# The last expert stage of a two-layer transformer kernel, moved into the attention's block of instructions

## The chip, the cores and the metric

The kernel runs on one core of a Trainium2 chip. The metric is the time of the whole kernel in microseconds of the device. The engines are TensorE (PE), VectorE (DVE), ScalarE (ACT), GpSimd (POOL) and SyncE (SP); each takes its own instructions in order and waits for the others by semaphores.

## What is computed

Four residual layers run over x, which is 4 batches of 512 rows by 512:

```python
x = x + tanh(g_xattn[0]) * _L0_xattn_ref(_layernorm(x), ...)
x = x + tanh(g_ffn[0])   * _L0_ffn_ref(_layernorm(x), ...)
x = x + tanh(g_xattn[1]) * _L1_xattn_ref(_layernorm(x), ctx, ...)   # attention, 32 heads of 16
x = x + tanh(g_ffn[1])   * _L1_ffn_ref(_layernorm(x), router_w, w1, w2, w3)
```

Only the last two matter here. The attention rotates queries and keys, takes a softmax over 512 keys, and projects by Wout. The last layer routes each row to two of eight experts with an inner size of 128:

```python
top_scores, selected = top_k(x_flat @ router_w.T, 2); top_scores = softmax(top_scores)
h = silu(xb @ w1[e]) * (xb @ w3[e])          # bfloat16 operands
out = sum over the two experts e of top_score[e] * (h @ w2[e])
```

The kernel computes all eight experts for every row and weighs them by gates that are zero for six of them.

## The kernel before

X (128 partitions by 16 tiles by 512) stays in SBUF throughout. Each layer is a function with its own block of instructions and its own SBUF buffers. A block begins when every engine has finished the one before.

`attention` (L1787) works on 16 units: unit (b, c) is 8 heads of batch b. An order written by hand sets everything. `turns` runs turn(b, c) for b from -1 to 3 and c from 0 to 3, and then turn(4, 0). A turn has 8 steps, each with two slots (slot 2n and 2n+1 belong to step n). In every step PE computes four score tiles of 128 keys by 512 queries (L2138), two before a slot and two after it, and ACT takes the exp of each (L2241); two PSUM banks hold the scores, so each score waits for the exp two before it. PE also takes products with the values (L2168), and for later units score rows whose maxima DVE takes (L2155, L2394). Small jobs go into the slots, as `jobs` lists them, and share PSUM bank 7: "x" transposes normalized rows, which ACT copies to xT (L2079, L2211); "q" projects queries; "m" turns maxima; "o" and "a" turn the attention's output (L2095, L2100) and "p" projects it with Wout (L2107), after which DVE adds it to X (L2384). PE starts a job only when the one before it is done (the table DONE). In the last two turns before (4, 0) much is missing: turn (3, 3) has neither "x", "q" nor "m" and no maxima, and turn (3, 2) has maxima in its first half alone. Turn (4, 0) has only the end of the last unit and sixteen "p" matmuls on four banks.

For each unit POOL stores the maxima and loads them again in another layout (L2056, L2065); the first scores of the unit wait for that load. SP loads keys, values and queries one to three turns ahead.

`l1_ffn` (L2403) is the last block. SP loads the router's weights (L2472). POOL makes constants and issues 17 loads of the experts' weights that turn float32 into bfloat16 on the way (L2488, L2489). DVE takes the row statistics and normalizes batches 0 and 1 (L2530, L2533, L2545), ACT the square roots (L2620). PE turns the normalized rows (L2689), ACT copies them to xT (L2632), POOL casts them to xb (L2496). PE multiplies by the router (L2695), ACT copies (L2637), PE sums the parts (L2701), DVE chooses two experts and makes the gates (L2561 to L2578) with one exp on ACT (L2624). These are the `first_jobs`. Then the loop over 16 tiles: two times `up` (L2715), silu (L2644), product (L2586), weighing by the gates on POOL (L2505), transposes (L2726), their copy (L2650), `down` (L2736), the sum into X (L2591) and the store. The next batch's "x", "l" and "s" jobs lie between these as `side_jobs`.

## Time and profile before

| | |
|---|---|
| median of 3 runs | 1400.13 us (1398.43 to 1401.13) |
| the profiled execution | 1398.27 us, of which the span is 1396.6 us |
| busy: PE, DVE, ACT, POOL | 83%, 62%, 47%, 30% |
| mean granted TensorE clock | 0.930 of full |
| attention's last x added | 1250.7 us |
| first expert matmul | 1273.2 us |

The span reaches from the first instruction to the last. Times in rows are microseconds from its start. The shares of busy time are averages over stages that differ; the stretch between the attention and the experts is read by itself.

### The profile page before, as it was taken

How to read it: one execution, taken by the hardware profiler on the slowest of the kernel's cores; microseconds unless marked ns; L12 is line 12 of the kernel's file. 1: busy time of each engine (PE TensorE's matmuls, PEld its weight loads, DVE VectorE, ACT ScalarE, POOL GpSimd, SP SyncE). 2: the span in 40 equal slices, each digit the busy share in tenths (PEclk: the TensorE clock that was granted, in tenths of full speed). 3: DMA queues.
4: the chain of work that ended last, by engine and by line, in shares of the span. 5: the costliest groups of instructions: out<-in, count | busy, mean ns of one | idle time of the engine just before them, and what ended most of it. 6: DMA issues, size and time to landing. Idle time of an engine off the chain costs nothing. (4 is left out here: it accounts for less than half of the span.)

```text
span 1396.6 us, 16561 instructions
## 1 busy us (share of the span) xinstructions
PE 1165.5 (83%) x5256; PEld 504.7 (36%) x5317; DVE 860.0 (62%) x1325; ACT 654.6 (47%) x1147; POOL 413.2 (30%) x479
## 2 busy tenths in 40 slices
PE   5775875999799999963459988998999999876897
PEld 3443432555444444431013222222322222223453
DVE  7899875214245555315798887778777777226543
ACT  2554452555322222241347666556655556724543
POOL 3475470010132222113334432222222220015332
...
DMA packets 106356, 141.58 MB, mean 101 GB/s; under 512 B 20788, under 2 KB 75572, under 8 KB 106280
## 3 DMA queue, kind: packets, MB, share of 16 engines
...
## 5 line engine op out<-in xcount | busy, mean ns | idle before, releaser
L2394 DVE TENSOR_REDUCE a_top<-PS 128x2 f32<-128x1024 f32 x256 | 308.4, 1222 | 94.8 <-PE PS L2155 90.8
L2241 ACT ACTIVATE a_E<-PS 128x512 f32<-128x512 f32 x512 | 277.7, 596 | 150.0 <-PE PS L2138 149.8
L2138 PE MATMUL PS<-a_Q,a_K 99*128 99x512 bf16 (+1 forms) x469 | 157.0, 386 | 16.6 <-ACT a_E L2241 6.2
L2155 PE MATMUL PS<-a_K,a_Q 64*128 64x512 bf16 x512 | 104.2, 405 | 48.9 <-DVE a_top L2394 29.6
L1367 PE MATMUL PS<-f_W,f_GT 128*128 x312 | 141.6, 597 | 0.0
L2168 PE MATMUL PS<-a_E,a_V 128*32 128x512 f32 x1024 | 136.9, 607 | 0.4 <-ACT a_E L2241 0.4
L2138 PEld LDWEIGHTS PS<-a_Q,a_K 99*128 99x128 bf16 (+1 forms) x512 | 44.2, 97 | 155.4 <-ACT a_E L2241 105.4
L1771 POOL TENSOR_TENSOR a_qf<-a_qf,a_tab 128x512 f32<-128x512 f32 x15 | 19.1, 1270 | 269.3 <-DVE a_swapped L2338 269.3
L1423 DVE TENSOR_TENSOR f_H<-f_SG,PS 128x256 f32<-128x256 f32 x39 | 16.4, 421 | 125.2 <-ACT f_SG L1407 125.2
L1367 PEld LDWEIGHTS PS<-f_W,f_GT 128*128 128x128 f32 x312 | 56.9, 192 | 57.2 <-issue 57.2
L2155 PEld LDWEIGHTS PS<-a_K,a_Q 64*128 64x128 bf16 x512 | 24.7, 93 | 141.9 <-issue 72.4
L2083 PE MATMUL PS<-a_xT,a_wq 128*128 128x512 f32 x128 | 73.9, 675 | 2.1 <-ACT a_xT L2211 0.8
L1386 PE MATMUL PS<-f_W,f_HT 128*128 x156 | 73.2, 593 | 0.0
L2107 PE MATMUL PS<-a_wo,a_attnT 128*128 128x512 f32 x128 | 66.8, 626 | 0.8 <-ACT a_attnT L2231 0.8
L1407 ACT ACTIVATE f_SG<-PS 128x256 f32<-128x256 f32 x39 | 15.0, 384 | 110.0 <-PE PS L1367 110.0
L2715 PE MATMUL PS<-f_W,f_xb 128*128 128x512 bf16 x249 | 62.2, 392 | 0.6 <-issue 0.2
L953 PE MATMUL PS<-f_W,f0r_xT 128*128 128x512 f32 x128 | 58.3, 598 | 0.0
L2505 POOL TENSOR_TENSOR f_H<-f_HF,f_gates 128x512 bf16<-128x512 f32 x32 | 33.3, 1039 | 73.9 <-DVE f_HF L2586 73.9
L1413 ACT COPY f_Y<-PS 128x512 f32<-128x512 f32 x39 | 22.8, 585 | 60.4 <-PE PS L1386 60.4
L2586 DVE TENSOR_TENSOR f_HF<-f_SG,PS 128x512 f32<-128x512 f32 x32 | 22.0, 688 | 47.3 <-ACT f_SG L2644 47.2
L1330 POOL COPY f_idx<-f_token_of 128x1 int32 (+1 forms) x39 | 13.1, 336 | 125.1 <-PE PS L1347 118.0
L1333 POOL DMA_INDIRECT f_G<-f_xn,f_idx x39 | 41.4, 1061 | 29.5 <-POOL f_idx L1330 29.5
...
## 6 DMA issues: line engine op xcount, KB each, us to landing
...
```

Source lines behind the costliest of these rows:

```text
L953: last = nc.tensor.matmul(PS[:, 5, 0:2 * I], xT[b % 2][:, c, t * P:(t + 1) * P], W13[:, E, c, :], start=(c == 0), stop=(c == DC - 1))
L1333: pool.indirect_dma_start(out=G[k][:], out_offset=None, in_=xn_dram, in_offset=bass.IndirectOffsetOnAxis(ap=idx[:, k:k + 1].bitcast(U32), ...
L1367: last = nc.tensor.matmul(PS[:, 2 + k % 2, 0:2 * I], GT[k][:, c, :], W13[:, bass.ds(e, 1), c, :].rearrange("p a n -> p (a n)"), start=(c = ...
L1386: last = nc.tensor.matmul(PS[:, 6 + k % 2, :], HT[k][:, c, :], W2[:, bass.ds(e, 1), c, :].rearrange("p a n -> p (a n)"), start=(c == 0), s ...
L2083: last = nc.tensor.matmul(B, wq[:, extra, c * P:(c + 1) * P], xT[:, extra, :], start=(extra == 0), stop=(extra == DC - 1))
L2107: last = nc.tensor.matmul(bank_of(kind, unit, extra), attnT[b % 2][:, d, t * P:(t + 1) * P], wo[:, d, :], start=(d == 0), stop=(d == DC - 1))
L2138: nc.tensor.matmul(PS[:, 4 + h % 2, :], K6[k][0:rows_, o, head // 2, kt * P:(kt + 1) * P], Q6[k][0:rows_, o, head // 2, :], start=True, st ...
L2155: last = nc.tensor.matmul(PS[:, 2 * pair + o, :], Q6[k][at, o, h // 2, t * P:(t + 1) * P], K6[k][at, o, h // 2, :], start=True, stop=True)
L2168: last = nc.tensor.matmul(PS[32 * h:32 * h + 32, 6, :], V[k][:, kt, (step // 4) * 4 + h, :], E[step % 2][:, h, :], start=(kt == 0), stop=( ...
L2241: nc.scalar.activation(E[step % 2][:, h, :], PS[:, 4 + h % 2, :], ACT.Exp).then_inc(exp_done, 1)
L2394: nc.vector.tensor_reduce(top[:, h - h % 2:h - h % 2 + 2, t], PS[:, 2 * pair:2 * pair + 2, :], AX.X, ALU.max).then_inc(maxed, 1)
L2715: last = nc.tensor.matmul(PS[:, 2 * h + m, :], xb[b % 2][:, c, t * P:(t + 1) * P], W13[:, c, m, h * HE:(h + 1) * HE, :].rearrange("p e i - ...
```

## The change

The last stage becomes a class, `LastStage`, whose parts are called from the attention's block. There is no block of its own any more.

- Buffers: it has none of its own. The up weights lie over Wq and the attention's normalized rows (now one buffer, `early`), the down weights over the keys of ring place 0, the cast rows over the queries of place 0, normalized rows of both batches over place 1, the loop's temporaries over place 2, small things over the rotation table.
- POOL issues 8 weight loads after its work of turn (3, 0), 8 after that of turn (3, 1), and the down weights and the constants after that of turn (3, 2). It casts batch 0's rows in turn (3, 3).
- DVE takes the statistics of batches 0 and 1 at slot 8 of turn (3, 2) and normalizes them at slot 12. ACT takes the square roots at the head of step 6 of that turn.
- In turn (3, 3) the jobs "ex" (slots 0 to 3), "el" (slot 5) and "es" (slot 7) turn the rows, multiply by the router and sum. DVE makes the gates from slot 7 on.
- Then each engine goes on to the loop over tiles (`tensor_main` and so on), whose text is the old one except for two waits of PE for the attention's last sums (`tiles_added`). The last projections use bank 6 in place of bank 0.

```diff
@@ -97,8 +97,7 @@
-        l1_ffn(nc, X, PS, identf, identb, tg, ln_eps, before, ones_b, router_w, w1, w2, w3, out)
+                  (weights, pos, ys, tg[:, 2:3]), (router_w, w1, w2, w3, out))
...
+class LastStage:
...
+    def __init__(self, nc, sem, X, PS, identf, identb, tg, ln_eps, ffn, early, xT, Q6, K6, tab, qf, swapped):
...
+        self.W13 = early[:].rearrange("p a c d -> p (a c d)").bitcast(BF16).rearrange("p (c m e i) -> p c m e i", c=DC, m=2, e=E)
+        self.W2T = K6[0][:].rearrange("p o h s -> p (o h s)").rearrange("p (e d) -> p e d", e=E)
+        self.xT = xT
+        self.xb = [Q6[0][:, k].rearrange("p h s -> p (h s)").rearrange("p (c n) -> p c n", c=DC) for k in range(2)]
+        self.xh = [Z[:].rearrange("p o h s -> p (o h s)").bitcast(F32).rearrange("p (t d) -> p t d", t=TB) for Z in (Q6[1], K6[1])]
+        work = [Q6[2][:].rearrange("p o h s -> p (o h s)"), K6[2][:].rearrange("p o h s -> p (o h s)")]
...
+        self.lT = qf[:, 0, :]
...
+    def sync(self, sp):
+        sp.dma_start(self.rw, self.router_w).then_inc(self.rw_loaded, 16)
...
+    def pool_load_up(self, pool, h):
+        for e in range(h * self.HE, (h + 1) * self.HE):
+            for m, w in enumerate((self.w1, self.w3)):
+                pool.dma_start(self.W13[:, :, m, e, :], w[e].rearrange("(c p) i -> p c i", p=P)).then_inc(self.w13_loaded[h], 16)
...
+    def pool_constants(self, pool):
+        pool.memset(self.rwT, 0.0).then_inc(self.consts_ready, 1)
...
+    def cast(self, pool, b, c):
+        pool.wait_ge(self.xT_ready, b * self.DC + c + 1)
+        if b >= 2:
+            pool.wait_ge(self.up_done, 2 * self.TB * (b - 1))
+        pool.nop(nofuse=True)
+        self.nc.gpsimd.tensor_scalar(self.xb[b % 2][:, c, :], self.xT[:, c, :], 1.0, 0.0, ALU.mult, ALU.add).then_inc(self.xb_ready, 1)
...
+    def constants(self, v):
+        for c in range(self.DC):
...
+    def statistics(self, v, b, n=1):
+        tiles = range(b * self.TB, (b + n) * self.TB)
+        done = b * self.TB
+        for t in tiles:
+            self.nc.vector.bn_stats(self.stats[:, t % (2 * self.TB), :], self.X[:, t, :]).then_inc(self.steps_norm, 1)
+        v.wait_ge(self.steps_norm, done + n * self.TB)
+        for t in tiles:
...
+    def normalize(self, v, b):
+        if b >= 2:
...
+    def choose(self, v, b):
...
+    def root(self, act, b, n=2):
+        act.wait_ge(self.var_ready, b + n)
+        self.nc.scalar.activation(self.sd[:, self.tiles(b, n)], self.mv[:, self.tiles(b, n), 1], ACT.Sqrt, bias=self.ln_eps[:]).then_inc(self.sd_ready, n)
+    def expo(self, act, b):
+        act.wait_ge(self.shifted_ready, b + 1)
+        self.nc.scalar.activation(self.ex, self.shifted, ACT.Exp).then_inc(self.ex_ready, 1)
+    def take_x(self, act, b, c):
+        if (b, c) == (0, 0):
+            act.wait_ge(self.rw_turned, 1)
+            act.wait_ge(self.consts_ready, 3)
+            self.nc.scalar.copy(self.rwT[:, :, 0:self.E], self.SIDE[:, 0:self.DC * self.E].rearrange("p (c e) -> p c e", e=self.E)).then_inc(self.rwT_ready, 1)
+        act.wait_ge(self.x_turned, b * self.DC + c + 1)
+        if b:
+            act.wait_ge(self.xb_ready, (b - 1) * self.DC + c + 1)
+            act.wait_ge(self.l_done, b)
+        self.nc.scalar.copy(self.xT[:, c, :], self.SIDE).then_inc(self.xT_ready, 1)
...
+    def turn_x(self, pe, b, c):
+        nc = self.nc
+        if (b, c) == (0, 0):
+            pe.wait_ge(self.rw_loaded, 16)
+            for d in range(self.DC):
+                last = nc.tensor.transpose(self.SIDE[:, d * self.E:(d + 1) * self.E], self.rw[:, d * P:(d + 1) * P], self.identf[0:self.E, 0:self.E])
+            last.then_inc(self.rw_turned, 1)
...
+            if b:
+                pe.wait_ge(self.logits_taken, b)
+        else:
+            pe.wait_ge(self.xT_ready, b * self.DC + c)
+        for t in range(self.TB):
+            last = nc.tensor.transpose(self.SIDE[:, t * P:(t + 1) * P], self.xh[b % 2][:, t, c * P:(c + 1) * P], self.identf[:])
...
+    def router(self, pe, b):
...
+    def router_sums(self, pe, b):
...
+    def tensor_main(self, pe, tiles_added):
+        nc, PS, TB, DC, E, HE, NT = self.nc, self.PS, self.TB, self.DC, self.E, self.HE, self.NT
+        def job(kind, b, c):
+            if kind == "x":
+                if (b, c) == (1, 0):
+                    pe.wait_ge(tiles_added, NT - 3)
...
+        def turn_h(j):
+            pe.wait_ge(self.h_ready, 2 * j + 2)
+            if j:
+                pe.wait_ge(self.hT_ready, j)
+            else:
+                pe.wait_ge(tiles_added, NT)
...
+def attention(nc, X, PS, identf, identb, ones_b, tg, ln_eps, tgate, Wq, Wout, bout, tables_dram, k_parts, v_dram, routed,
+              ffn):
...
-        wq = sb("wq", [P, DC, D])
+        early = sb("early", [P, 2, DC, D])
+        wq, xh = early[:, 0], early[:, 1]
...
-        xh = sb("xh", [P, TB, D])
...
+            if (b, c) == (NB - 1, DC - 1):
+                for d in range(DC):
+                    add(d, "ex", (0, 0), d)
+                add(5, "el", (0, 0))
+                add(7, "es", (0, 0))
...
-            return PS[:, (7, 4, 5, 0)[extra[0]], :] if kind == "p" and unit[0] == NB - 1 else PS[:, 7, :]
+            return PS[:, (7, 4, 5, 6)[extra[0]], :] if kind == "p" and unit[0] == NB - 1 else PS[:, 7, :]
...
             turns(sp, turn)
+            sp.wait_ge(parts_ready, NU)
+            f1.sync(sp)
...
+            def load_last_stage(b, c):
+                if (b, c) == (NB - 1, 0):
+                    pool.wait_ge(q_turned, NU)
+                    pool.wait_ge(x_turned, NB * DC)
+                    f1.pool_load_up(pool, 0)
+                if (b, c) == (NB - 1, 1):
+                    f1.pool_load_up(pool, 1)
+                if (b, c) == (NB - 1, 2):
+                    pool.wait_ge(st_done, n_st((NB - 1, 0), 7, 3))
+                    f1.pool_load_down(pool)
+                    pool.wait_ge(parts_ready, NU)
+                    f1.pool_constants(pool)
+                if (b, c) == (NB - 1, DC - 1):
+                    f1.pool_first(pool)
...
+                load_last_stage(b, c)
             turns(pool, turn)
+            f1.pool_main(pool)
...
+                if kind == "ex":
+                    f1.turn_x(pe, b, extra)
+                if kind == "el":
+                    f1.router(pe, b)
+                if kind == "es":
+                    f1.router_sums(pe, b)
...
+                    "a": (aT_ready, lambda u, e: n_unit(u)), "p": (x_added, lambda u, e: u[0] * TB + e[0] + 1),
+                    "ex": (f1.xT_ready, lambda u, e: e + 1), "el": (f1.lT_ready, lambda u, e: 1), "es": (f1.logits_taken, lambda u, e: 1)}
...
             turns(pe, turn)
+            pe.wait_ge(maxed, NU * HU * 2)
+            f1.tensor_main(pe, x_added)
...
+                        if kind == "ex":
+                            f1.take_x(act, unit[0], extra)
+                        if kind == "el":
+                            f1.take_router(act, unit[0])
+                        if kind == "es":
+                            f1.expo(act, unit[0])
...
+                    if (b, c, step) == (NB - 1, 2, 6):
+                        f1.root(act, 0)
                     exps((b, c), step, (0, 1))
...
             turns(act, turn)
+            act.wait_ge(st_done, n_st((NB - 1, 2), 7, 3))
+            f1.scalar_main(act)
...
+                if (b, c) == (NB - 1, 2):
+                    def first_rows():
+                        v.wait_ge(x_added, 2 * TB)
+                        v.wait_ge(parts_ready, NU)
+                        f1.statistics(v, 0, 2)
+                    def first_normalized():
+                        v.wait_ge(st_done, n_st((NB - 1, 1), 7, 3))
+                        f1.row_roots(v, 0)
+                        f1.normalize(v, 0)
+                        f1.normalize(v, 1)
+                    at(8, first_rows)
+                    at(12, first_normalized)
+                if (b, c) == (NB - 1, DC - 1):
+                    def first_gates():
+                        v.wait_ge(qf_ready, NU)
+                        f1.constants(v)
+                        f1.choose(v, 0)
+                    at(7, first_gates)
...
-def l1_ffn(nc, X, PS, identf, identb, tg, ln_eps, before, ones_b, router_w, w1, w2, w3, out):
...
```

The order of instructions shows where the parts went. PE in turn (3, 3), before, from the last "p" of turn (3, 2) to the job "a"; Q_3 and K_3 are scores, E and V values:

```order
L2107 MATMUL PS<-a_wo,a_attnT 128x512
L2138 MATMUL PS<-a_Q_3,a_K_3 128x512 x4
L2168 MATMUL PS<-a_E,a_V 32x512 x4
L2138 MATMUL PS<-a_Q_3,a_K_3 128x512 x4
L2168 MATMUL PS<-a_E,a_V 32x512 x4
L2138 MATMUL PS<-a_Q_3,a_K_3 128x512 x2
L2095 MATMUL PS<-identf,a_OT 128x128 x4
```

The same place on PE in the changed kernel (L2086 turns the router's weights, L2096 the normalized rows, which lie in Q_1):

```order
L2534 MATMUL PS<-a_wo,a_attnT 128x512
L2566 MATMUL PS<-a_Q_3,a_K_3 128x512 x2
L2086 MATMUL PS<-identf,a_tab 128x8 x4
L2096 MATMUL PS<-identf,a_Q_1 128x128 x4
L2566 MATMUL PS<-a_Q_3,a_K_3 128x512 x2
L2596 MATMUL PS<-a_E,a_V 32x512 x4
L2096 MATMUL PS<-identf,a_Q_1 128x128 x4
L2566 MATMUL PS<-a_Q_3,a_K_3 128x512 x2
L2096 MATMUL PS<-identf,a_Q_1 128x128 x4
L2566 MATMUL PS<-a_Q_3,a_K_3 128x512 x2
L2596 MATMUL PS<-a_E,a_V 32x512 x4
L2096 MATMUL PS<-identf,a_Q_1 128x128 x4
```

Four groups of transposes and the turning of the router's weights have moved between the scores. PE at the end of the attention, before, up to the first expert matmuls:

```order
L2107 MATMUL PS<-a_wo,a_attnT 128x512 x16
L1810 UNCONDITIONAL_BRANCH
L2673 UNCONDITIONAL_BRANCH
L2677 MATMUL PS<-identf,f_rw 128x8 x4
L2689 MATMUL PS<-identf,f_xh 128x128 x16
L2695 MATMUL PS<-f_xT,f_rwT 32x512 x4
L2701 MATMUL PS<-f_pick,f_lT 128x8 x4
L2715 MATMUL PS<-f_W,f_xb 128x512 x8
```

And in the changed kernel (L2137 is `up`, with the weights in `early`):

```order
L2534 MATMUL PS<-a_wo,a_attnT 128x512 x16
L2137 MATMUL PS<-a_early,a_Q_0 128x512 x8
L2096 MATMUL PS<-identf,a_K_1 128x128 x4
L2137 MATMUL PS<-a_early,a_Q_0 128x512 x8
L2096 MATMUL PS<-identf,a_K_1 128x128 x4
```

The branch into a new block and 28 matmuls ahead of the first expert matmul are gone from there. ACT in the changed kernel, from step 5 of turn (3, 2) to the choice of batch 0's experts (L2677 the attention's exps, L2020 square root, L2035 copies to xT, L2041 the copy behind the router, L2024 the gates' exp):

```order
L2677 ACTIVATE a_E<-PS 128x512 x4
L2020 ACT_TABLE_LOAD
L2020 ACTIVATE a_tab<-a_tab,ln_eps 128x8
L2677 ACT_TABLE_LOAD
L2677 ACTIVATE a_E<-PS 128x512 x10
L2030 COPY a_tab<-PS 128x4x8
L2035 COPY a_xT<-PS 128x512
L2677 ACTIVATE a_E<-PS 128x512 x2
L2686 COPY a_OT<-PS 128x512
L2035 COPY a_xT<-PS 128x512
L2677 ACTIVATE a_E<-PS 128x512 x2
L2035 COPY a_xT<-PS 128x512
```

Two table loads and a square root now stand between exps of the attention, and the copies between those of turn (3, 3).

## Rows read from the trace of the kernel before

**Rows 1.** Stretches: from:to, length, busy PE PEld DVE ACT POOL (count), clock, DMA, GB/s.

```profile
1178.50:1205.60 27.10, 24.96 (x134) 7.48 (x136) 12.77 (x18) 19.27 (x36) 1.62 (x3) 1.00 0.01 2
1205.60:1231.50 25.90, 23.04 (x119) 6.78 (x123) 2.26 (x6) 18.71 (x35) 0.00 (x0) 1.00 0.00 1
1231.50:1250.00 18.50, 15.96 (x48) 6.83 (x40) 3.57 (x7) 1.17 (x2) 0.00 (x0) 1.00 0.00 0
1250.00:1273.20 23.20, 8.65 (x37) 5.25 (x39) 13.55 (x32) 6.16 (x10) 15.93 (x24) 0.61 1.21 136
```

**Rows 2.** Timeline of PE: start, us, engine, line, out<-in, xcount [idle before <-releaser].

```profile
1235.96 13.97 PE L2107 MATMUL PS<-a_wo,a_attnT 128*128 128x512 f32 x32 [0.77 <-ACT a_attnT L2231]
...
1253.83 0.41 PE L2677 MATMUL PS<-identf,f_rw 8*128 8x8 f32 x4 [3.90 <-DMA f_rw<-in_L_ffn_router_w_dram]
1259.20 1.11 PE L2689 MATMUL PS<-identf,f_xh 128*128 128x128 f32 x4 [4.96 <-DVE f_xh L2545]
...
1268.40 1.93 PE L2695 MATMUL PS<-f_xT,f_rwT 128*32 128x512 f32 x8 [0.77 <-ACT f_xT L2632]
1271.12 1.85 PE L2701 MATMUL PS<-f_pick,f_lT 128*128 128x8 f32 x8 [0.79 <-ACT f_lT L2637]
1273.20 2.85 PE L2715 MATMUL PS<-f_W,f_xb 128*128 128x512 bf16 x7 [0.23 <-issue]
...
1276.32 1.89 PE L2715 MATMUL PS<-f_W,f_xb 128*128 128x512 bf16 x8
1281.06 0.65 PE L2689 MATMUL PS<-identf,f_xh 128*128 128x128 f32 x4 [2.85 <-ACT f_xT L2632]
```

**Rows 3.** Timeline of ACT, around a square root in turn (1, 3).

```profile
959.47 1.28 ACT L2256 ACT_TABLE_LOAD   x1
960.76 0.30 ACT L2256 ACTIVATE a_sd<-a_mv,ln_eps 128x4 f32<-128x4 f32 x1
961.08 1.28 ACT L2241 ACT_TABLE_LOAD   x1
```

**Rows 4.** Timeline of ACT, turns (3, 2) and (3, 3), steps before the tail.

```profile
1195.58 2.15 ACT L2241 ACTIVATE a_E<-PS 128x512 f32<-128x512 f32 x4
1198.45 1.08 ACT L2241 ACTIVATE a_E<-PS 128x512 f32<-128x512 f32 x2 [0.71 <-PE PS L2138]
...
1206.12 2.17 ACT L2241 ACTIVATE a_E<-PS 128x512 f32<-128x512 f32 x4 [1.46 <-PE PS L2138]
...
1212.09 2.17 ACT L2241 ACTIVATE a_E<-PS 128x512 f32<-128x512 f32 x4 [0.72 <-PE PS L2138]
```

**Rows 5.** Timeline of ACT, turn (2, 0), steps 4 and 5 with jobs "x".

```profile
1000.65 0.58 ACT L2211 COPY a_xT<-PS 128x512 f32<-128x512 f32 x1 [0.92 <-PE PS L2079]
1001.13 1.09 ACT L2241 ACTIVATE a_E<-PS 128x512 f32<-128x512 f32 x2
...
1005.02 1.06 ACT L2241 ACTIVATE a_E<-PS 128x512 f32<-128x512 f32 x2
```

**Rows 6.** Timelines of DVE and ACT: "o" of turn (3, 2), and the last stage.

```profile
1196.49 0.26 DVE L2372 RECIPROCAL a_rsum<-PS 128x16 f32<-128x16 f32 x1 [3.44 <-PE PS L2095]
...
1252.97 2.46 DVE L2530 BATCH_NORM_STATS2 f_stats<-X 128x6 f32<-128x512 f32 x4
1255.47 0.38 DVE L2533 BATCH_NORM_AGGREGATE f_mv<-f_stats 128x2 f32<-128x6 f32 x4
...
1262.65 3.31 DVE L2545 TENSOR_SCALAR f_xh<-X,f_mv,f_rstd 128x512 f32<-128x512 f32 x4
...
1273.75 0.23 ACT L2624 ACTIVATE f_ex<-f_shifted 128x32 f32<-128x32 f32 x1 [1.47 <-DVE f_shifted L2564]
```

**Rows 7.** Timeline of POOL: loads of maxima, and the first weight loads.

```profile
1140.63 1.12 POOL L2065 DMA_DIRECT2D a_Q<-a_m_rows  x2 [3.02 <-DMA a_m_rows<-a_mT]
1167.21 0.54 POOL L2056 DMA_DIRECT2D a_m_rows<-a_mT  x1 [25.47 <-ACT a_mT L2222]
...
1252.86 11.96 POOL L2488 DMA_DIRECT2D f_W<-in_L_ffn_w_dram  x16
```

586 lines of the change are left out of this document (267 added, 319 removed).

## The prediction, made before the changed kernel ran

> **What bounds the kernel now.** I read the busy time by stretch first, then the timeline of PE between the attention and the experts, then ACT in the attention's last two units, and last DVE and POOL there. In the table of stretches [rows 1] the reader is to see one poor stretch, 1250.00 to 1273.20: PE is busy for 8.65 of 23.2 us at a granted clock of 0.61, and the DMA share is 1.21. All around it the clock is 1.00. The timeline of PE [rows 2] says what stands there: after the last projections (1235.96 plus 13.97, so 1249.93) PE waits 3.90 us for the router's weights and 4.96 us for the normalized rows, then goes through transposes, router and sums, each waiting for an ACT copy, and starts the first expert matmul at 1273.20. It then runs without a long wait for the weights (0.23 us of "issue"). So the 23.3 us from 1249.93 to 1273.20 are a chain of small steps, with the weight loads of POOL beside it [rows 7].
>
> **What is removed.** In the changed order `up` of tile 0 stands right behind the sixteen projections on PE. All that it needs is made earlier: weights in turns (3, 0) and (3, 1), cast rows in turn (3, 3). The gates are needed only by POOL's weighing. The two waits for the attention's sums hide: the first transposes of batch 1 want 13 of 16 tiles, the first `turn_h` all 16, and DVE's last sum ends under 1 us behind the last projection, while `turn_h` stands behind two `up`. The whole 23.3 us go, block boundary included.
>
> The clock goes with them. The first `up` took 2.85 us, the second, at the full clock, 1.89 us [rows 2]: that is 0.96 us. What follows, PE's 2.85 us of waiting for the copy at 1281.06, stays: the chain of silu, product, statistics of batch 2, root and copy is unchanged, only DVE is no longer busy with gates. So the loop gains 1.0 us, and 1.2 if the clock doesn't dip behind that wait. Removed in all: 24.3 us.
>
> **What is added to the attention, step by step.** There ACT's exps and PE's scores take turns, so what stands between them is on the path, less what was idle.
>
> (1) Square roots at the head of step 6 of turn (3, 2). The same pair of table loads stands in turn (1, 3): from 959.47 to 961.08 plus 1.28, 2.9 us for load, root and load [rows 3]. ACT was idle for 0.71 us before that step [rows 4]. Cost 2.2 us. Is its input there? DVE is free after the maxima are cut (1196.49 less 3.44 of waiting, so 1193.1), and eight tiles of statistics are twice 2.46 plus 0.38, 5.7 us [rows 6], so to 1198.8; ACT wants it at 1195.58 plus 2.15 plus a load of 1.28, at 1199.0. It just is. The statistics stand ahead of "o", which DVE did at 1196.49 [rows 6]; it slips by some 2.3 us, and PE's next job with it to about 1199.7, but the scores then wait for ACT until past 1200.6 anyway: no cost. The normalization is two times up to 3.31 us [rows 6], from 1199.5 to at most 1206.3; DVE's next duty is the sum at 1206 plus 2.2. No cost either. The cover is thin here: 1 us more on DVE would show as 1 us.
>
> The Trainium skill, in "ScalarE: Activation LUTs", section "What ACT_TABLE_LOAD costs", gives 1283 ns for a load and some 2.66 us for a switch with the drain behind it. The trace agrees with the first and not with the second: 1.28 us, and the next instruction starts at once [rows 3]. By the page's figure this step would cost two times 2.66 plus 0.30 less 0.71, an estimate of 4.9 us, and the forecast would be 2.7 us later.
>
> (2) The jobs "ex" in slots 0 to 3 of turn (3, 3), with the router's weights in the first. Step 0 and step 1 took 5.97 us together, 1206.12 to 1212.09 [rows 4]. The nearest row is a step of turn (2, 0) with two "x" jobs: 3.9 us with maxima, 1001.13 to 1005.02 [rows 5]; two of them are 7.8, 1.8 more. Here the router's weights come on top. Following the semaphores: PE turns the router's weights (0.41, [rows 2]), waits for ACT's copy, turns rows (half of 1.11 at the full clock), ACT copies (0.58, [rows 5]) and takes its exps; the next "ex" waits for that copy. I get 8.6 us for the two steps, so 2.6 us more.
>
> (3) "el" in slot 5: PE's 1.93 us were at half clock, so 0.97, then ACT's copy of 0.58, for which step 3 waits. ACT had 0.72 us idle a step [rows 4]. I get 1.4 us with the semaphores. (4) "es" in slot 7: half of 1.85, then DVE's copy, maximum and difference, then ACT's exp. From the end of PE's sums (1272.97) to the end of that exp (1273.75 plus 0.23, [rows 2, 6]) is 1.0 us. 1.9 us in a row, of which ACT's idle time and its running exps hide some: 1.0 us.
>
> Sum: 2.2 + 2.6 + 1.4 + 1.0 = 7.2 us. Bounds: nothing hidden gives 2.9 for (1), 0.6 plus four times (0.56 + 0.58) for (2), 5.2, then 1.9 for (3) with a semaphore's delay, and 1.9 for (4), so 11.9 us. At the other end PE's jobs hide under ACT's work and ACT's copies in its idle time: 0.2 + 5 x 0.58 + 0.23 is 3.3 us of ACT, and five steps have 5 x 0.72, 3.6 us, so only the 2.2 us of (1) stay. I take the value between, since it follows the waits one by one; rows 5 show that such copies do not hide whole.
>
> (5) POOL's issues: 16 in 11.96 us, 6 us in each of two turns [rows 7]. POOL has 25.47 us of waiting ahead of the next store of maxima [rows 7], so it is not late. SP is past its loads for the last unit. (6) Casts, constants, and the bank taken instead of bank 0: nobody waits for POOL there. Cost nothing.
>
> **The sum.** 24.3 less 7.2 is 17.1 us. The profiled execution took 1398.27 us, its span 1396.6, so it would take 1381.2. It was faster than the median by 1.9 us and stands just below the three timed runs; against the median of 1400.13 the same difference gives **1383.0 us**, which I predict.
>
> **Rivals.** (A) The transfers collide. The weights are halves of 2 MB read; the whole took from 1252.86 to 1273, with a DMA share of 1.21 [rows 1, 7], so some 10 us a half. POOL issues each half right behind the loads of maxima (issued 1140.63 to 1141.8, wanted by the scores at about 1149), and if their pieces share engines with the weights they land up to 10.6 us later, at 1152.4: 3 us of waiting, twice. Against it: they are ahead in POOL's order, and the transfers of the last two units are nearly none (share 0.01, [rows 1]). The Trainium skill ("DMA: Bandwidth & Descriptors", "Queues, rings and completion order") says that each DMA engine takes the queues in turn, and one queue in its order: by that the earlier loads lose little. It would give 17.1 less 6.3, so 10.8 us of gain: 1389.3 us.
>
> (B) The handshakes run in series, the upper bound above: 24.3 less 11.9 is 12.4 us: 1387.7 us.
>
> (C) Slower than before: the clock. The new jobs put waits of PE, up to 1.2 us each, into turn (3, 3). PE's work there and in the tail is 23.04 plus 15.96 us, 39 us, in 44.4 us [rows 1]. If the granted clock fell to its lower level (1.2 GHz) at the start of that turn and stayed there, 78 us would be needed: 34 us more, against 17.1, so 1417 us. It decides from about 17 us of PE's full-clock work run at half. Against it: at 23.04 busy of 25.90 us the clock was 1.00 throughout, and the projections run without a gap [rows 1, 2]; the only lower clocks follow stretches in which PE did next to nothing.
>
> (D) The change doesn't do what it says: `up` of tile 0 still waits, for the casts or the weights. POOL would have to be 45 us late; the rows show it idle for 25 us a turn. Or the loop gains more than I count, from DVE and ACT that have less to do. Either is small.
>
> **How the numbers follow.** Forecast, a gain of 12.5 to 22.1 us about 17.1: 0.78. (B) or beyond, down to 11 us: 0.08. (A): 0.08. (C): 0.03. (D): 0.03, half of it on the fast side. The added cost between 2.2 and 11.9 us puts the time between 1378.0 and 1387.7; with (A) it reaches 1389.3, and the three runs spread by about 1 us each way. Range 1378 to 1390. About 0.2% is what a measurement of this kernel tells from no change, 2.8 us: faster 0.96, within it 0.01, slower 0.03.
>
> **What would show it.** In the profile after: the first expert matmul within 0.5 us of the last projection, at about 1257; eight of them in 1.9 us; clock 1.00 from there. ACT's load, root and load in 2.9 us before step 6 of turn (3, 2), the exps following at about 1200.6. Steps 0 and 1 of turn (3, 3) in 8.6 us, steps 2 and 3 in 5.8 plus 2.4. A "p" or a score that waits for DVE in turn (3, 2) would say that the statistics are late; a first score of turns (3, 1) or (3, 2) that waits for a DMA would say (A); a clock below 1.00 before the last projection, (C). The forecast is wrong if turns (3, 2) and (3, 3) together grow by less than 2 or more than 12 us.

## The result, and the profile after

| | before | changed |
|---|---|---|
| median of 5 runs | 1401.13 us (1398.43 to 1403.46) | **1390.31 us** (1388.06 to 1394.82) |
| ratio | | 0.9925, 95% interval 0.9904 to 0.9946 |
| the profiled execution | 1398.27 us, span 1396.6 | 1388.06 us, span 1386.4 |
| busy: PE, DVE, ACT, POOL | 83%, 62%, 47%, 30% | 85%, 62%, 47%, 30% |
| mean granted TensorE clock | 0.930 | 0.931 |

The kernel is faster by about 10.5 us. The prediction had 17.1, and its range ended at 1390.0: the direction was right, the size was not. A second measurement gave 1391.30 us, a ratio of 0.9932 (0.9918 to 0.9946); one slow execution of the kernel before in it, 1902.83 us at a granted clock of 0.60, is not counted.

In the changed kernel L2020 is the square root, L2677 the attention's exps, L2035 the copies to xT, L2566 the scores, L2596 the values, L2534 Wout, L2137 `up`, L2160 `down`, L2057 silu. First the table of stretches of the changed kernel, with the columns of [rows 1]:

```profile
1196.00:1204.00 8.00, 5.32 (x32) 1.59 (x24) 6.69 (x21) 6.59 (x11) 2.96 (x5) 1.00 0.03 7
1204.00:1208.00 4.00, 3.67 (x12) 0.94 (x13) 2.74 (x7) 1.85 (x4) 0.99 (x3) 0.57 0.89 119
...
1247.00:1262.00 15.00, 14.79 (x37) 6.58 (x38) 3.00 (x4) 0.07 (x1) 0.00 (x0) 1.00 0.00 1
1262.00:1275.00 13.00, 8.75 (x46) 4.81 (x44) 5.16 (x13) 7.98 (x11) 3.58 (x5) 0.87 0.00 0
```

The poor stretch at clock 0.61 [rows 1] is gone. A new short one stands at 1204 to 1208, inside turn (3, 2), at a granted clock of 0.57. From 1262 to 1275 the clock is 0.87 with PE busy for 8.75 of 13 us; the loop had such a dip before too, as is shown further down. PE's timeline shows what stands at the old boundary and behind it:

```profile
1247.21 13.97 PE L2534 MATMUL PS<-a_wo,a_attnT 128*128 128x512 f32 x32 [0.77 <-ACT a_attnT L2667]
1261.02 1.89 PE L2137 MATMUL PS<-a_early,a_Q 128*128 128x512 bf16 x8
...
1263.19 1.89 PE L2137 MATMUL PS<-a_early,a_Q 128*128 128x512 bf16 x8
1269.33 1.12 PE L2096 MATMUL PS<-identf,a_K 128*128 128x128 f32 x4 [4.25 <-ACT a_xT L2035]
1270.24 3.04 PE L2137 MATMUL PS<-a_early,a_Q 128*128 128x512 bf16 x8
...
1378.44 3.53 PE L2160 MATMUL PS<-a_K,a_K 128*128 128x512 bf16 x8 [1.10 <-ACT a_K L2063]
```

The first `up` follows the projections with no wait, at full clock, as predicted: compare the rows from 1235.96 to 1273.20 in [rows 2]. PE then waits 4.25 us in the loop instead of 2.85, does its third `up` in 3.04 us, and its last `down` takes 3.53 us. ACT in the attention, and where its tables are loaded:

```profile
1197.67 2.15 ACT L2677 ACTIVATE a_E<-PS 128x512 f32<-128x512 f32 x4
1200.77 1.28 ACT L2020 ACT_TABLE_LOAD   x1 [0.95 <-DVE a_tab L1937]
1202.06 0.30 ACT L2020 ACTIVATE a_tab<-a_tab,ln_eps 128x8 f32<-128x8 f32 x1
1202.38 1.28 ACT L2677 ACT_TABLE_LOAD   x1
1203.68 1.08 ACT L2677 ACTIVATE a_E<-PS 128x512 f32<-128x512 f32 x2
...
1208.82 1.09 ACT L2677 ACTIVATE a_E<-PS 128x512 f32<-128x512 f32 x2 [2.76 <-PE PS L2566]
...
1229.00 0.23 ACT L2024 ACTIVATE a_tab<-a_tab 128x32 f32<-128x32 f32 x1 [1.74 <-DVE a_tab L1971]
...
1262.99 1.28 ACT L2057 ACT_TABLE_LOAD   x1 [15.92 <-PE PS L2137]
1264.29 0.60 ACT L2057 ACTIVATE a_Q<-PS 128x512 f32<-128x512 f32 x1
```

Two loads of tables stand *behind* a wait that belongs to the operation after them: the root's (0.95 us for DVE's variances) and silu's (until PE has done `up`).

**Where the 17.1 went.** The first exp of step 5 of turn (3, 2) is a common point: 1195.58 before [rows 4], 1197.67 after. The kernels differ only behind it on the path, so all is counted from there; the 2.09 us ahead of it are taken up below.

| stretch, from the exps of step 5 on | before | after | difference | predicted |
|---|---|---|---|---|
| to step 6 (roots) | 2.87 | 6.01 | +3.14 | +2.2 |
| from there to step 7 | 3.84 | 5.14 | +1.30 | 0 |
| steps 0 and 1 of turn (3, 3) ("ex") | 5.97 | 8.11 | +2.14 | +2.6 |
| step 2 ("el") | 2.88 | 3.94 | +1.06 | +1.4 |
| step 3 ("es") | 2.89 | 4.44 | +1.55 | +1.0 |
| all to the start of the last projections | 40.38 | 49.54 | +9.16 | +7.2 |
| from their start to the first `up` | 37.24 | 13.81 | -23.43 | -23.3 |
| from the first `up` to the sixth | 19.79 | 20.14 | +0.35 | -1.0 |
| from there to the end of the span | 103.61 | 105.24 | +1.63 | 0 |
| sum | 201.02 | 188.73 | -12.29 | -17.1 |

The change is worth 12.29 us in this pair; 2.09 us less show because the profiled execution was later at step 5 already. Of the missing 4.8 us, 0.94 are the roots, 1.30 a step at a low clock and 2.98 the loop. Against these stand 0.25 that the three kinds of job cost less than predicted and 0.13 that the boundary gave more.

### The profile page after: what moved, and what is told of

Same layout as the page of the kernel before. It is cut to its first block, busy times and chain, and to the rows that moved or that the text cites. A ratio compares the mean times of both kernels' runs of the same rounds, so it can differ in the third digit from the quotient of the medians.

```text
span 1386.4 us, 16598 instructions
## 1 busy us (share of the span) xinstructions
PE 1177.1 (85%) x5316; PEld 503.8 (36%) x5317; DVE 856.9 (62%) x1324; ACT 653.6 (47%) x1146; POOL 414.5 (30%) x479
## 4 chain that ended last, share of the span: by engine, by line
PE 30%; DVE 8%; issue 7%; ACT 6%; POOL 2%; DMA 2%; POOLq 0%; ACTq 0%; DVEq 0%
PE PS L2596 8%; PE PS L2566 6%; PE PS L2510 5%; PE PS L2534 5%; ACT a_E L2677 4%; PE PS L2583 4%; DVE a_top L2854 3%; POOL a_K L1908 1%; DMA a_attnT<-f_y,l_pos 1%; PE PS L2137 1%; DVE a_tab L1934 1%; DVE a_early L2756 1%; PE PS L2160 1%; PE PS L2506 0%; PE PS L2527 0%
## 5 line engine op out<-in xcount | busy, mean ns | idle before, releaser
L2677 ACT ACTIVATE a_E<-PS 128x512 f32<-128x512 f32 x512 | 277.7, 596 | 148.2 <-PE PS L2566 147.9
L2566 PE MATMUL PS<-a_Q,a_K 99*128 99x512 bf16 (+1 forms) x512 | 168.0, 388 | 17.9 <-ACT a_E L2677 7.8
L2596 PE MATMUL PS<-a_E,a_V 128*32 128x512 f32 x1024 | 139.0, 615 | 0.0
L2566 PEld LDWEIGHTS PS<-a_Q,a_K 99*128 99x128 bf16 (+1 forms) x512 | 44.5, 98 | 154.6 <-ACT a_E L2677 102.3
L2510 PE MATMUL PS<-a_xT,a_early 128*128 128x512 f32 x128 | 75.6, 689 | 2.1 <-ACT a_xT L2647 0.8
L2534 PE MATMUL PS<-a_wo,a_attnT 128*128 128x512 f32 x128 | 67.1, 629 | 1.4 <-ACT a_attnT L2667 0.8
L1908 POOL TENSOR_TENSOR a_K<-a_Q,a_tab 128x512 bf16<-128x512 f32 x32 | 33.3, 1041 | 109.0 <-DVE a_Q L1996 109.0
L2137 PE MATMUL PS<-a_early,a_Q 128*128 128x512 bf16 x256 | 61.6, 384 | 0.0
L1996 DVE TENSOR_TENSOR a_Q<-a_Q,PS 128x512 f32<-128x512 f32 x32 | 22.0, 687 | 50.4 <-ACT a_Q L2057 50.4
```

What stands on the lines that cost most here:

```text
L1908: self.nc.gpsimd.tensor_tensor(self.H[j % 2][:, h * HE:(h + 1) * HE, :], self.HF[h], gate, ALU.mult).then_inc(self.h_ready, 1)
L2137: last = nc.tensor.matmul(PS[:, 2 * h + m, :], self.xb[b % 2][:, c, t * P:(t + 1) * P], self.W13[:, c, m, h * HE:(h + 1) * HE, :].rearrang ...
L2510: last = nc.tensor.matmul(B, wq[:, extra, c * P:(c + 1) * P], xT[:, extra, :], start=(extra == 0), stop=(extra == DC - 1))
L2534: last = nc.tensor.matmul(bank_of(kind, unit, extra), attnT[b % 2][:, d, t * P:(t + 1) * P], wo[:, d, :], start=(d == 0), stop=(d == DC - 1))
L2566: nc.tensor.matmul(PS[:, 4 + h % 2, :], K6[k][0:rows_, o, head // 2, kt * P:(kt + 1) * P], Q6[k][0:rows_, o, head // 2, :], start=True, st ...
L2596: last = nc.tensor.matmul(PS[32 * h:32 * h + 32, 6, :], V[k][:, kt, (step // 4) * 4 + h, :], E[step % 2][:, h, :], start=(kt == 0), stop=( ...
```

## Experiments

The figures "from step 5" below are in the same measure as the table. Each kernel is the changed one with one edit, but for the first and the last four.

**The kernel before, a second time.** It asks how much of the difference of 2.09 us ahead of step 5 is the kernel's.

> The kernel before, unchanged, for a second trace. In the traced pair the changed kernel is already 2.1 us late in step 5 of turn (3, 2) of the attention (1197.67 against 1195.58), ahead of every instruction that the change added, weight loads apart. Theory (chance): this is the spread of one execution against another, in the stages that wait for DMAs; then this second trace has that step at 1195.6 plus or minus up to 3 us, and the distance from there to the first expert matmul and to the end is the same within 0.5 us (77.6 and 201.0 us). Rival (layout): the changed buffers cost 2 us ahead of the attention; then this trace stands within 0.7 us of 1195.6, and all changed kernels stand near 1197.7.

1399.99 us, span 1398.3. The exps of step 5:

```profile
1197.30 2.15 ACT L2241 ACTIVATE a_E<-PS 128x512 f32<-128x512 f32 x4
```

That is 1.72 us later than in the first profile [rows 4], while everything from there on is the same to 0.02 us: 40.37 to the projections, 77.62 to the first `up`, 123.38 to the end. So times counted from step 5 compare kernels to some hundredths of a microsecond wherever the clock is the same, and the place of step 5 itself is a matter of the execution. In all thirteen profiles of this study step 5 lies between 1195.6 and 1202.6, and most of that spread stands already at the square root of turn (1, 3), at 960.8 to 967.8 [rows 3], ahead of all instructions that the change or an experiment moves.

**The root counted once.** Its semaphore rises by two at once, for two batches. In the trace above the wait for the variances stands in front of the table load and not of the root. That is the exception: in the changed kernel's whole trace only two other loads stand behind a wait, silu's and one at 9.41 us, and at both the program has two waits in a row. At all other places where an operation has to wait, its load runs first and the operation waits. The edit asks whether the increment by two is the reason here.

```diff
-ACT.Sqrt, bias=self.ln_eps[:]).then_inc(self.sd_ready, n)
+ACT.Sqrt, bias=self.ln_eps[:]).then_inc(self.sd_ready, 1)
...
-        v.wait_ge(self.sd_ready, b + n)
+        v.wait_ge(self.sd_ready, b + n - 1)
```

> The square roots' semaphore is raised once by one in place of by two, and its reader waits for one less; nothing else changes. By that the wait for the variances stands on the square root and the table load goes ahead of it. Theory: in turn (3, 2) the load starts at the end of step 5's exps (1199.8 on the scale of the changed kernel's trace) and no longer waits 0.95 us for DVE, so step 6 begins 5.0 us after the last exps of step 5 began in place of 6.0, and with PE's idle time shorter by 0.9 the clock may not dip (then 1.3 us more are gained by step 7). Rival: DVE is late anyhow, and the gain is below 0.5 us.

1385.01 us in one run. ACT:

```profile
1196.57 2.15 ACT L2677 ACTIVATE a_E<-PS 128x512 f32<-128x512 f32 x4
1198.74 1.28 ACT L2020 ACT_TABLE_LOAD   x1
1200.03 0.30 ACT L2020 ACTIVATE a_tab<-a_tab,ln_eps 128x8 f32<-128x8 f32 x1
1200.35 1.28 ACT L2677 ACT_TABLE_LOAD   x1
1201.65 2.17 ACT L2677 ACTIVATE a_E<-PS 128x512 f32<-128x512 f32 x4
```

The load starts right behind the exps, and step 6 comes 5.08 us behind step 5: 0.93 us less, the 0.95 us of the wait. Against the 2.87 us of the kernel before, load, root and load now cost 2.21 us, the 2.2 us of the prediction. The next step took 3.83 us, not 5.14. Both together put the projections 2.22 us earlier (47.32).

**PE kept at work during the roots.** The table's 1.30 us ahead of step 7 have a granted clock of 0.57 around them. Three causes are possible: the low clock, DVE, which normalizes there, or the load of the down weights, which starts there (119 GB/s from 1204 to 1208). Eight unused matmuls fill PE's wait.

```diff
+                    if (b, c, step) == (NB - 1, 2, 6):
+                        pe.wait_ge(maxed, NU * HU * 2)
+                        for _ in range(8):
+                            nc.tensor.matmul(PS[:, 0, :], K6[2][0:99, 0, 0, 0:P], Q6[2][0:99, 0, 0, :], start=True, stop=True)
                     scores((b, c), step, 2)
```

> Eight matmuls of 128x512 bf16 whose results nobody uses are added on PE in step 6 of turn (3, 2), where it idled for 1.86 us while ACT loads tables; nothing else changes, the square roots' 3.1 us stay. Theory (clock): the granted clock fell to its lower level there because PE did next to nothing for 2 us, the values of that step took 1.94 in place of 1.07 us, and step 7 came 1.3 us late. With PE at work the clock stays at 1.00, the values take 1.07 us and step 7 begins 3.8 to 3.9 us after step 6 in place of 5.14. Rival (weights): the down weights' load, which starts there, slows PE; then the values still take 1.9 us and step 7 stays 5.1 us behind.

1390.76 us. PE, in the changed kernel and then in this one:

```profile
1204.33 1.09 PE L2566 MATMUL PS<-a_Q,a_K 99*128 99x512 bf16 x2 [1.86 <-ACT a_E L2677]
1205.36 1.94 PE L2596 MATMUL PS<-a_E,a_V 128*32 128x512 f32 x8
```

```profile
1204.32 1.89 PE L2609 MATMUL PS<-a_Q,a_K 99*128 99x512 bf16 x8
...
1207.15 1.06 PE L2596 MATMUL PS<-a_E,a_V 128*32 128x512 f32 x8
```

The values matmuls take 1.06 us instead of 1.94, step 6 is where it was (6.00) and step 7 is 3.84 us behind it, the figure of the kernel before. DVE's work and the weights' load are unchanged. So the 1.30 us were the clock, behind a wait of PE of 1.86 us, and neither of the other two had a part. Yet the run as a whole won nothing: its last projections took 15.2 us instead of 13.8 (15.4 as the records stand, but that of one matmul of the first `up` is missing), at a granted clock of 0.73 and 0.70 in the six microseconds from 1246 on. That is a low clock at another place, of which more below.

**The router behind the projections.** Batch 0's turning, router, sums and gates leave turn (3, 3) and stand between the last projection and `up`; weights and rows stay where the change put them.

```diff
-                for d in range(DC):
-                    add(d, "ex", (0, 0), d)
-                add(5, "el", (0, 0))
-                add(7, "es", (0, 0))
...
+            pe.wait_ge(x_added, NT - 3)
+            for d in range(DC):
+                f1.turn_x(pe, 0, d)
+            f1.router(pe, 0)
+            f1.router_sums(pe, 0)
             f1.tensor_main(pe, x_added)
```

> One part of the change undone: batch 0's transposes, router, sums and gates stand behind the last projections on all engines again (as in the kernel before), while weights, statistics, square roots and normalized rows stay in the attention's last batch. Times below are from the start of step 5 of turn (3, 2). Changed kernel: projections at 49.54 us, first expert matmul at 63.35. Theory (the steps add as read): turn (3, 3) is free of its 4.9 us, so projections at 44.8 (43.4 without the clock's dip in turn (3, 2)); then the chain runs at the full clock in 4 x (0.56 + 0.68) + 0.8 + 0.6 + 0.97 + 0.7 + 0.93, some 9 us, so the first expert matmul at 67 to 68: 4 us later than in the changed kernel. Rival (the jobs in the attention hide nothing): it comes at 63.4 or before, and placing them there was worth nothing.

1391.37 us. The projections start 45.12 us behind step 5, 4.42 us earlier than in the changed kernel, so that is what the jobs cost in turn (3, 3). The chain between the last projection and the first `up`:

```profile
1254.95 0.41 PE L2086 MATMUL PS<-identf,a_tab 8*128 8x8 f32 x4
...
1261.56 1.94 PE L2102 MATMUL PS<-a_xT,a_tab 128*32 128x512 f32 x8 [0.68 <-ACT a_xT L2035]
1264.29 1.84 PE L2110 MATMUL PS<-a_tab,a_qf 128*128 128x8 f32 x8 [0.80 <-ACT a_qf L2041]
1265.99 3.38 PE L2137 MATMUL PS<-a_early,a_Q 128*128 128x512 bf16 x8
```

It takes 11.1 us (11.04 by the starts), above the 9 expected, because the clock falls in it: the router's 1.94 us and `up`'s 3.38 us are at the lower level of 1.2 GHz. The first `up` is at 70.06, later than the 67 to 68 that were expected. So moving the router into the attention is worth 70.06 less 63.35, 6.7 us at the first `up`, and all the rest (weights, rows, the block's boundary) 77.62 less 70.06, 7.6 us. The loop gave some back to this kernel (123.71 against 125.38): silu's table could be loaded while the slow `up` ran. The whole is 5.0 us by the profiles (1.67 less than the 6.7).

**Silu's table load.** At the end of the attention ACT has two waits in a row, for the last scores and for the first `up`. One of them is carried by the table load. The first is implied by the exps before it and can go.

```diff
             turns(act, turn)
-            act.wait_ge(st_done, n_st((NB - 1, 2), 7, 3))
             f1.scalar_main(act)
```

> One wait of ACT is left out that earlier waits of ACT already cover, the one on the scores of turn (3, 2) ahead of the loop over tiles; nothing else changes. In the changed kernel the load of silu's table stands behind the wait for the first expert matmuls: PE ends at 1262.91, the load takes 1.28 us, silu starts at 1264.29. Theory (load behind its wait): with one wait in place of two the load goes ahead of it, silu starts about 0.1 us after the matmuls, and the second group of transposes of batch 1 comes at 7.0 us after the first expert matmul in place of 8.3; the loop after tile 4 is 1.3 us nearer. Rival: the load's time is not what sets that place (statistics or copies do), and it moves by less than 0.5 us.

1392.95 us in one run, but in it step 5 was at 1202.59, the latest of all. Counted from the first `up`, the rest took 121.85 us instead of 125.38. ACT now, and the last `down`:

```profile
1252.30 1.28 ACT L2057 ACT_TABLE_LOAD   x1
1271.16 0.60 ACT L2057 ACTIVATE a_Q<-PS 128x512 f32<-128x512 f32 x1 [17.58 <-PE PS L2137]
```

```profile
1384.96 1.90 PE L2160 MATMUL PS<-a_K,a_K 128*128 128x512 bf16 x8 [1.10 <-ACT a_K L2063]
```

The load is done under the projections. The sixth `up` is 1.6 us earlier (1.8 as the records stand, but that of one matmul is missing at the first `up`). PE's wait shrank from 4.25 to 2.92 us, which is the load's 1.28, and the transposes and third `up` behind it were 0.23 us shorter; the last `down` takes 1.90 us as in the kernel before, not 3.53. Here too the projections were slow, by 3.0 us: 0.65 was the clock from 1249 to 1258, against 1.00 in the changed kernel at about the same place.

```profile
1249.00:1258.00 9.00, 6.83 (x15) 3.34 (x16) 0.68 (x2) 2.23 (x3) 0.00 (x0) 0.65 0.01 2
```

```profile
1243.00:1252.00 9.00, 6.53 (x27) 3.03 (x20) 1.79 (x4) 1.17 (x2) 0.00 (x0) 1.00 0.01 2
```

**PE kept at work in the loop.** Twelve unused matmuls behind the second `up`, four ahead of the last `down`.

```diff
+            if j == 0:
+                pe.wait_ge(tiles_added, NT)
+                for _ in range(12):
+                    nc.tensor.matmul(PS[:, 6, :], self.xb[0][:, 0, 0:P], self.W13[:, 0, 0, 0:HE, :].rearrange("p e i -> p (e i)"), start=True, stop=True)
             for one in self.side_jobs(b, t, 1):
                 job(*one)
```

> Twelve matmuls of 128x512 bf16 without use are added behind the second group of tile 0, where PE waits 4.25 us for a copy, and four ahead of the last tile's product, where it waits 1.1 us; nothing else changes. Theory (clock): the lower clock behind those waits goes (the third group of expert matmuls took 3.04 in place of 1.89 us, the last product 3.53 in place of 1.89), so from the first expert matmul to the end it takes 125.4 less 1.2 to 2.8 us: 122.6 to 124.2. Rival: both dips were hidden by other waits; then it stays at 125.4.

1388.34 us. From the first `up` to the end 123.62 us, 1.76 us less than in the changed kernel. Of these, 0.45 stand at the sixth `up`, where the third now takes 1.89 us, and 1.31 behind it. This is the end of the loop:

```profile
1379.07 1.03 PE L2181 MATMUL PS<-a_early,a_Q 128*128 128x512 bf16 x4
1380.34 1.90 PE L2160 MATMUL PS<-a_K,a_K 128*128 128x512 bf16 x8 [0.24 <-ACT a_K L2063]
```

More work on PE made the loop shorter; the `down` that follows the unused matmuls takes 1.90 us. From step 6 to step 7 of turn (3, 2), untouched here, it took 5.49 us, so the slow step came again (5.14 in the changed kernel, 3.84 before).

**The statistics spread over turn (3, 1).** DVE takes one tile's statistics in each of slots 1 to 8 of turn (3, 1), ACT the root before step 7 of it, and the normalization moves to slot 8 of turn (3, 2). It asks whether the roots cost less where more matmuls (those for the maxima) stand beside them.

```diff
+                    for t in range(2 * TB):
+                        at(t + 1, lambda t=t: one_row(t))
+                    at(10, rows_done)
...
-                    if (b, c, step) == (NB - 1, 2, 6):
+                    if (b, c, step) == (NB - 1, 1, 7):
                         f1.root(act, 0)
```

> Statistics of batches 0 and 1 are taken one tile in a slot in turn (3, 1) in place of eight at once in turn (3, 2); the square roots stand ahead of step 7 of turn (3, 1), where ACT waits 1.7 us for PE in every step, and the rows are normalized from slot 8 of turn (3, 2). Theory: in turn (3, 2) steps 5, 6, 7 and the next are as in the kernel before (2.87, 3.84, 3.83 us), which gives back 4.4 us there; turn (3, 1) grows by 2.9 less 1.7, so 1.2 us, plus what 5.7 us of statistics cost DVE, which has 6.9 us of waiting in that turn: 0 to 2 us. Net 1.5 to 3 us better than the changed kernel. Rival: DVE bounds turn (3, 1) through the maxima, the turn grows by 5 us or more, and nothing is gained.

1384.67 us in one run. Turn (3, 2) is back at the figures of before, 2.86 us to step 6 and 3.84 from there to step 7, and the projections start at 45.17: 4.37 us less. ACT in turn (3, 1):

```profile
1174.67 1.28 ACT L2020 ACT_TABLE_LOAD   x1
...
1176.29 1.28 ACT L2677 ACT_TABLE_LOAD   x1
1177.58 2.16 ACT L2677 ACTIVATE a_E<-PS 128x512 f32<-128x512 f32 x4
```

Turn (3, 1) grew from 29.34 to 30.92 us, so 1.58 us are paid for the same 2.9 us of loads and root: ACT had more idle time to give there (in the kernel before it waited 1.72 us for PE ahead of step 7, against 0.71 ahead of step 6 of turn (3, 2)). The net is 2.8 us less.

**What is best together.** Three kernels with 5 rounds on one chip: the changed kernel again; the root counted once, silu's load and the spread statistics in one; and the same with the unused matmuls in the loop.

> The changed kernel, unaltered, a second time. If the figures of the first profile are its own: 1388 to 1392 us, step 6 of turn (3, 2) 6.0 us behind step 5, first expert matmul 63.3 us behind step 5, and 125.4 us from there to the end of the span. The theory of the clock (it falls behind stretches in which PE waits, and not always by the same amount) lets the single sums of 1.3, 1.1 and 1.6 us come out otherwise, up to 2 us each way in all, while the waits for tables and copies must come out the same within 0.1 us.

> Three edits together: root counted once (its table load ahead of the wait), statistics of batches 0 and 1 spread over turn (3, 1) with the root there, and silu's table load ahead of the wait by taking away the second wait. If their gains add: rows in turn (3, 1) gave 4.4 less 1.6, 2.8 us; silu's load is worth 3.5 us in the loop, of which the clock in the projections took 3.0 back in its single run. So 2.8 + 0.5 to 2.8 + 3.5, and about 0.5 for the root: 3.8 to 6.8 us faster than the changed kernel, 1383.5 to 1386.5 us at a median of 1390.3. The rival, that each such gain only moves a dip of the clock elsewhere: within 2 us of the run with the rows in turn (3, 1) alone, and no faster than 1387.

> The run before, plus the unused matmuls in the loop (12 behind the first up of the second half, 4 ahead of the last down), all on PE. If the lower clock behind PE's waits is what costs there: 1 to 2 us less than the run without them (alone they gave 1.8). The rival, that silu's earlier load has already taken that cost away (its own run had no dip before the last down): 0 to 0.9 us more, since PE has more to do.

| | median, us | all | ratio to before |
|---|---|---|---|
| changed kernel | 1391.30 | 1390.09 to 1392.89 | 0.9932 (0.9918 to 0.9946) |
| three edits | 1383.64 | 1378.87 to 1386.71 | 0.9862 (0.9842 to 0.9883) |
| three edits and unused matmuls | 1380.79 | 1378.88 to 1384.23 | 0.9859 (0.9841 to 0.9877) |

The changed kernel repeats: 6.01 to step 6, 63.68 to the first `up` (0.33 more, of which 0.31 stand between steps 6 and 7, at the low clock), 125.51 from there. The three edits are worth 7.7 us by the medians of this measurement, above the 3.8 to 6.8 expected; the time itself, 1383.64 us, lies at the lower end of the 1383.5 to 1386.5 forecast. This version beats both kernels clearly. Whether the unused matmuls add anything is not settled: the medians say 2.9 us, the ratios 0.4, and the intervals overlap nearly whole. From the first `up` to the end the profiles give 122.05 us without and 120.62 with them.

The profile with three edits was its slowest execution, and shows why. First its stretches, then those of the kernel with the unused matmuls, where all comes 1.9 us earlier:

```profile
1240.00:1243.00 3.00, 2.20 (x15) 0.51 (x11) 0.75 (x1) 0.59 (x1) 0.00 (x0) 1.00 0.00 0
1243.00:1246.00 3.00, 1.33 (x9) 0.91 (x9) 0.68 (x2) 0.81 (x2) 0.00 (x0) 0.87 0.00 0
1246.00:1249.00 3.00, 3.00 (x4) 1.38 (x5) 0.00 (x0) 1.05 (x1) 0.00 (x0) 0.50 0.02 5
1249.00:1252.00 3.00, 3.00 (x4) 1.01 (x3) 0.00 (x0) 0.00 (x0) 0.00 (x0) 0.50 0.00 0
```

```profile
1240.00:1243.00 3.00, 1.30 (x12) 0.84 (x8) 0.80 (x3) 0.58 (x1) 0.00 (x0) 1.00 0.00 0
1243.00:1246.00 3.00, 2.23 (x7) 1.06 (x6) 0.00 (x0) 1.87 (x2) 0.00 (x0) 1.00 0.02 5
1246.00:1249.00 3.00, 3.00 (x8) 1.33 (x7) 0.75 (x1) 0.00 (x0) 0.00 (x0) 1.00 0.00 0
```

The instructions here are the same, and so are PE's waits for the tail's small steps, 0.80, 0.90 and 0.77 us. In one execution the granted clock falls to the lower level when the projections start and stays there for some 6 us, in the other it doesn't. It costs 3.04 us (16.85 against 13.81 us from the start of the projections to the first `up`). Of the twelve profiles without matmuls added in this tail, it fell in three: here, in the run with silu's load, and in the one with the filled root.

**PE kept at work in the tail too.** Three unused matmuls ahead of each of the three small steps.

```diff
+                        if b == NB and (kind in ("o", "a") or kind == "p" and extra == (0, 0)):
+                            pe.wait_ge(maxed, NU * HU * 2)
+                            pe.wait_ge(f1.xb_ready, DC)
+                            pe.wait_ge(f1.w13_loaded[0], 16 * 2 * f1.HE)
+                            for _ in range(3):
+                                nc.tensor.matmul(PS[:, 0, :], f1.xb[0][:, 0, 0:P], f1.W13[:, 0, 0, 0:f1.HE, :].rearrange("p e i -> p (e i)"), start=True, stop=True)
```

> The combined kernel with the unused matmuls in the loop, and three more unused matmuls on PE ahead of each of the three small steps of the attention's tail (the two transposes and the first projection), where PE works 1.3 of 3 us. If the sparse stretch there is what lets the clock fall at the projections in some executions (3.0 us in one profile of the combined kernel, none in the other with the same instructions): no execution more than 1.5 us above the fastest, median 1379 to 1380.5 us, and 58.9 us from step 5 to the first expert matmul in the profile. The fill itself fits into waits of 0.80, 0.90 and 0.77 us, 0.65 us each, so it costs at most 0.3 us. The rival, that the fall comes by chance and not from the sparse stretch: the spread stays at 4 us or more, as it was without this fill (1378.9 to 1384.2).

1381.75 us (1381.19 to 1386.91), ratio 0.9880 (0.9859 to 0.9902). The fill fits into the waits: 58.98 to the first `up`, and PE is busy for 2.96 and 2.63 of 3 us where it was busy for 1.30 and 2.23.

```profile
1240.00:1243.00 3.00, 2.96 (x16) 0.78 (x16) 0.75 (x1) 0.58 (x1) 0.00 (x0) 1.00 0.00 0
1243.00:1246.00 3.00, 2.63 (x15) 1.34 (x13) 0.68 (x2) 1.08 (x2) 0.00 (x0) 1.00 0.00 0
```

But the spread of the five runs is 5.7 us, more than the 4 us named for the rival, and the median is not lower. So the expectation fell: either falls of the clock at the projections are not the main part of the spread, or this fill does not prevent them. Only one of the five executions has a profile. It agrees with the profile of the kernel without this fill to 0.02 us up to the first `up` and to 0.04 us behind it, and yet its span is longer by 1.7 us, nearly all of it ahead of step 5. That speaks for the first, but one profile can't show that something never happens: whether this fill prevents the fall stays open.

## Why the prediction was wrong in size

**What bounds the kernel, and what is removed: right.** 23.43 us went at the boundary, 23.3 were predicted, and the first `up` ran at full clock.

**(1) The roots: the value right, the wait misplaced, 0.94 us.** 2.2 us were predicted and 2.21 measured once the root's load no longer carries the wait. The text let ACT load its table first and then wait for DVE, "It just is". The arrival was timed well: DVE's variances were there at 1200.69, 3.0 us behind the exps of step 5; predicted were 1198.8 less 1195.58, so 3.2:

```profile
1195.17 4.84 DVE L1934 BATCH_NORM_STATS2 a_tab<-X 128x6 f32<-128x512 f32 x8
1200.05 0.64 DVE L1937 BATCH_NORM_AGGREGATE a_tab<-a_tab 128x2 f32<-128x6 f32 x8
```

But with the wait on the load, the load must follow the variances and 0.94 us are added. The step that failed is "ACT wants it at 1195.58 plus 2.15 plus a load of 1.28": ACT wanted it before that load. DVE's further work hid, as predicted: PE's next "p" waited 0.63 us for it (1201.35), while the scores waited for ACT anyway; the normalization took 2.17 and 1.91 us, less than the 3.31 each that were allowed.

**The clock in the attention: put at nothing, 1.30 us.** The prediction weighed only one fall, (C), that lasts through turn (3, 3) and the tail. What came was short: PE waited 1.86 us for ACT's table loads, and about 3 us of work ran at the lower level. It came in all five profiles that have this wait and no fill (3.84 us became 5.14 to 5.49), and not where the wait was 0.93 us, with the root counted once. The step that failed is the sentence "the only lower clocks follow stretches in which PE did next to nothing": at [rows 2] that was the only case there was, and a wait of under 2 us inside a busy stretch was taken for none. The Trainium skill, "TensorE: Matmul & The Clock Gate", section "A second HAM failure mode: psum-queue depth-cycling", tells of a kernel whose clock swings between its levels because of short idles of PE between groups of matmuls. The page's idles are many; here a single wait of 1.86 us stood ahead of the fall, and filling it took the 1.30 us away.

**(2) to (4), the jobs: 4.75 us, predicted 5.0.** Following the semaphores one by one was near for the sum. "es" was under-sized, 1.55 for 1.0: ACT stood 1.74 us before the gates' exp, for DVE's copy, maximum and difference. The others were over-sized by 0.46 and 0.34.

**(5) The weight loads: right, rival (A) fell.** POOL issued the halves as predicted, 6.08 us for eight, right behind the loads of maxima:

```profile
1142.82 1.12 POOL L2484 DMA_DIRECT2D a_Q<-a_m_rows  x2 [3.10 <-DMA a_m_rows<-a_mT]
1143.93 6.08 POOL L1875 DMA_DIRECT2D a_early<-in_L_ffn_w_dram  x8
```

The offset between before and after is 2.09 us ahead of the first weight load (exps at 1140.03 and 1142.12), 2.09 at the first step of turn (3, 2) (1179.01 and 1181.10) and 2.09 at step 5 of it, and turn (3, 1) is 29.34 us long in both: nothing waited.

**The loop: the largest miss, 2.98 us.** It was to gain 1.0 and lost 1.98. The 1.0 came (the second `up` is 2.17 us behind the first, 3.12 before). The step that failed is the sentence "the chain of silu, product, statistics of batch 2, root and copy is unchanged". It isn't: before, the table for silu was loaded while `up` ran, and silu waited for `up` alone:

```profile
1274.00 1.28 ACT L2644 ACT_TABLE_LOAD   x1
1276.08 0.60 ACT L2644 ACTIVATE f_SG<-PS 128x512 f32<-128x512 f32 x1 [0.80 <-PE PS L2715]
```

The change put the wait of the attention's block in front of that load. So the load's 1.28 us were exposed, and PE's wait grew by 1.40 (4.25 for 2.85 us). That makes up the 1.35 us missing at the sixth `up`. The low clock behind this wait isn't new: the third `up` took 2.79 us in the kernel before, and from the transposes ahead of it to the fourth `up` it was 4.77 us before and 4.66 after.

```profile
1281.55 2.79 PE L2715 MATMUL PS<-f_W,f_xb 128*128 128x512 bf16 x8
```

The 1.63 us at the very end are a fall of the clock ahead of the last `down`, with the same waits of 0.80 and 1.10 us as before, where it didn't fall (1.90 us). This one is no accident of an execution: the last `down` took 3.22 to 3.57 us in all six profiles that have neither silu's load moved nor unused matmuls ahead of it (the changed kernel twice, the root counted once, the filled root, the spread statistics, the router behind), and 1.90 in both of before, in both with silu's load moved and no fill, and in the three with a fill. But the kernel with the router behind the projections has its silu load out of the way and the slow `down` none the less, so the late load isn't its cause by itself. The prediction had no term for it. Why the same waits fell at the end of one kernel and not of the other stays open.

**The rivals.** (B), handshakes in series, gave 11.9 us for the attention's part; 9.16 were measured, of which 6.92 without the load's wait and the clock. (C) in its form didn't come; two small falls did, of 1.30 us (ahead of step 7) and 1.63 us (the last `down`). (D) fell. The time, 1390.31, is nearest to (A)'s and (B)'s, for reasons that neither had.

**The base of the sum.** The prediction went by the first three runs of before, 1400.13 us; with all five it was 1401.13, and the measured ratios give 9.5 to 10.5 us for what the profiles from step 5 put at 11.8 and 12.3. A spread of some 5 us between executions, most of it there before turn (1, 3), lies over all of this.
